# Gated attention and a ternary feed-forward on one Trainium2 core: a third pair of w1's row blocks rounded by GpSimd, and new orders for all queues

## What is computed

```python
# attention: x is (4, 512, 512), ctx is (4, 512, 128)
adj  = layernorm(x)
si   = ctx @ Wi ; sj = ctx @ Wj
xatt = 0.6 * sigmoid(si[:, :, None] + sj[:, None, :] + b) + 0.4 * adj
x    = x + tanh(g_xattn) * xatt
# feed-forward on quantized operands
def bitlinear(x, w):
    xn = x * rsqrt(mean(x * x) + 1e-6)
    s  = 127 / max(abs(xn)) ; xq = clip(round(xn * s), -128, 127) / s
    t  = 1 / mean(abs(w))   ; wq = clip(round(w * t), -1, 1) / t
    return xq @ wq.T
h = silu(bitlinear(layernorm(x), w1)) * bitlinear(layernorm(x), w2)
x = x + tanh(g_ffn) * bitlinear(h, w3)
```

## Time and profile before

| | |
|---|---|
| median of 3 runs | 155.48 us |
| profiled execution, its own time | 154.29 us |
| its span, first to last instruction | 152.5 us |
| PE busy | 137.5 us, 90% |
| DVE busy | 118.8 us, 78% |
| POOL busy | 107.6 us, 71% |
| ACT busy | 103.8 us, 68% |
| granted TensorE clock | 1.00 of full speed |
| moved by DMA | 27.94 MB, mean 183 GB/s |

### The profile page before, as it was taken

One profiled execution on the slowest core, in us unless ns is written; L12 is line 12 of the kernel. 1 busy time (PEld: TensorE's weight loads), 2 busy tenths in 40 slices (PEclk: granted clock), 3 DMA queues, 4 the chain that ended last, 5 costly groups with the idle time before them and its releaser, 6 DMA issues.

```text
span 152.5 us, 2380 instructions
## 1 busy us (share of the span) xinstructions
PE 137.5 (90%) x711; PEld 75.6 (50%) x711; DVE 118.8 (78%) x179; ACT 103.8 (68%) x172; POOL 107.6 (71%) x158
## 2 busy tenths in 40 slices
PE   1379568989999999799999999999999999999992
PEld 1279557955554444344444444445454454444461
DVE  0235998999999999979999999992779468908742
ACT  3148599999989778977597794283919719572250
POOL 3021297999898489894998969999742985699420
PEclk9999999999999999999999999999999999999999
DMA  4899999996129569980469519255802195819773
GB/s 122 229 409 406 410 407 426 404 384 217 34 71 142 129 149 237 204 158 21 78 130 232 94 37 141 63 152 149 198 2 89 43 185 111 232 69 227 184 217 138
DMA packets 46004, 27.94 MB, mean 183 GB/s; under 512 B 37543, under 2 KB 37928, under 8 KB 45992
## 3 DMA queue, kind: packets, MB, share of 16 engines
q1 hardware_dynamic: 45696, 27.79, 68.1%
q10 hardware_dynamic: 296, 0.01, 0.1%
HBM read 14.55 MB, written 4.20 MB: 123 GB/s over the span
## 4 chain that ended last, share of the span: by engine, by line
PE 72%; ACT 11%; DMA 6%; issue 5%; POOL 3%; ACTq 1%; SPq 1%; DVE 1%; DVEq 0%; POOLq 0%
PE ps L1404 42%; PE ps L1441 23%; ACT junk L720 3%; DMA th_ring<-in_L_xattn_b_dram 3%; DMA xqT<-xq 2%; POOL hq L587 2%; PE ps L1436 2%; ACT w2T L725 1%; PE ps L1310 1%; ACT w1T L730 1%; ACT th_ring L775 1%; ACT junk_x L792 1%; ACT raw_room L805 1%; PE ps L1317 1%; ACT hqT L736 1%
## 5 line engine op out<-in xcount | busy, mean ns | idle before, releaser
L1404 PE MATMUL ps<-w1T,xqT 128*128 128x512 f16 (+1 forms) x192 | 40.7, 361 | 0.9 <-DMA xqT<-xq 0.9
L1404 PE MATMUL ps<-w2T,xqT 128*128 128x512 f16 (+1 forms) x192 | 40.7, 362 | 0.0
L1125 DVE SCALAR_TENSOR_TENSOR raw<-ps,deq,raw_room 128x1408 f32<-128x1408 f32 x16 | 26.9, 1683 | 14.2 <-PE ps L1404 14.1
L1441 PE MATMUL ps<-w3T,hqT 128*128 128x512 f16 x165 | 37.2, 379 | 0.3 <-issue 0.3
L805 ACT ACTIVATE raw_room<-ps,deq 128x1408 f32<-128x1408 f32 x16 | 22.9, 1433 | 14.9 <-PE ps L1404 14.9
L1404 PEld LDWEIGHTS ps<-w1T,xqT 128*128 128x128 f16 x192 | 18.6, 98 | 20.9 <-issue 1.6
L1404 PEld LDWEIGHTS ps<-w2T,xqT 128*128 128x128 f16 x192 | 18.3, 98 | 20.1 <-DVE raw L1125 1.2
L1132 DVE TENSOR_REDUCE h_top<-raw 128x1 f32<-128x1409 f32 x16 | 25.7, 1607 | 0.1
L587 POOL TENSOR_SCALAR hq<-raw,h_scale 128x1408 f16<-128x1408 f32 x15 | 22.6, 1506 | 4.4 <-DVE h_scale L1135 4.4
L1441 PEld LDWEIGHTS ps<-w3T,hqT 128*128 128x128 f16 x165 | 16.1, 98 | 19.0 <-issue 0.7
L816 ACT ACTIVATE junk<-raw 128x1410 f16<-128x1410 f32 x16 | 21.8, 1368 | 0.0
(11 more groups left out here) (106 smaller groups left out, 180.2 us busy)
## 6 DMA issues: line engine op xcount, KB each, us to landing
c_all<-in_x_dram SPq DMA_DIRECT2D x16, 256.0 KB, 10.0
out_dram<-out_ring SPq DMA_DIRECT2D x15, 256.0 KB, 2.5
raw<-in_L_ffn_w_dram SPq DMA_DIRECT2D x4, 704.0 KB, 12.7
raw_room<-in_L_ffn_w_dram SPq DMA_DIRECT2D x3, 768.0 KB, 8.6
raw<-in_L_ffn_w_dram SPq DMA_DIRECT2D x3, 768.0 KB, 11.7
hq<-in_ctx_dram SPq DMA_DIRECT2D x2, 256.0 KB, 6.2
raw_room<-in_L_ffn_w_dram SPq DMA_DIRECT2D x1, 512.0 KB, 10.7
raw<-in_L_ffn_w_dram SPq DMA_DIRECT2D x1, 512.0 KB, 11.7
```

Of the source, the lines that this page charges most:

```text
L1125: v.scalar_tensor_tensor(out=hid[:, t % HS, 0:H], in0=ps_up[:, 0:H], scalar=deq[:, 1, t:t + 1], in1=gate[:, t % GATES, :], op0=ALU.mult, o ...
L1404: last = m.matmul(bank[:, lo:hi], xqT[:, i % XT, k, :], wT[w][:, k, lo:hi], start=(k == 0), stop=(k == KD - 1))
L1441: last = m.matmul(ps_y[t % 2], hqT[:, t % HT, k, :], w3T[:, :, k, :], start=(k == 0), stop=(k == KH - 1))
```

## The change

A third pair of row blocks, 5 and 6, joins the pairs that POOL rounds and PE turns as half floats. `RAW`, the number of blocks turned as 32-bit floats, goes from 7 to 5, the second clip of w1 shrinks from three blocks to one, and the room `w1q` grows by two blocks. PE's transposes for these blocks are eight of half floats in place of eight of 32-bit floats; ACT loses `evac_rows(5)`, DVE's `evac_rows(6)` becomes the eviction of a pair, and POOL gains one `conv_rows`. The order lists of all five queues are new.

```diff
-    ROWS = [(t, t + 1) for t in range(7)] + [(7, 9), (9, 11)]
-    RAW = 7
+    ROWS = [(t, t + 1) for t in range(5)] + [(5, 7), (7, 9), (9, 11)]
+    RAW = 5
     CLIPS = [(0, 4), (4, RAW)]
-    ROWS_ACT = [0, 4, 5]
-    ROWS_DVE = [1, 2, 3, 6, 7, 8]
+    ROWS_ACT = [0, 4]
+    ROWS_DVE = [1, 2, 3, 5, 6, 7]
...
@@ SP
             load_x(11)
+            turn_x(2)
             load_x(12)
-            turn_x(2)
-            turn_x(3)
...
@@ PE
-                            rows_left([6, 7, 8][c])
+                            rows_left([6, 7, 7][c])
...
+            up_product(1)
             sum_w(2, "x", 2)
-            up_product(1)
...
+            gate_product(7)
             last_product(0)
-            gate_product(7)
```

More of the change, by code:

```diff
@@ L620, in _ @@
             affine_x(2)
+            quant_x(1)
             affine_x(3)
-            quant_x(1)
+            dequant_up(0)
+            dequant_gate(0)
+            step_x(1)
             hidden_floors()
-            dequant_up(0)
-            step_x(1)
-            ctx_product(2)
             dequant_x(1)
             quant_x(2)
+            ctx_product(2)
             slopes_x(3)
@@ L631, in _ @@
             step_x(2)
+            quant_h(0)
+            dequant_x(2)
             conv_w(2, 0)
-            dequant_x(2)
+            quant_x(4)
             conv_w(2, 1)
-            quant_x(4)
-            conv_w(2, 2)
-            mean_x(0)
             quant_x(5)
             step_x(3)
+            conv_w(2, 2)
             dequant_x(3)
-            quant_h(0)
+            dequant_h(0)
+            quant_x(6)
+            mean_x(0)
+            conv_w(2, 3)
             quant_h(1)
-            quant_x(6)
-            conv_w(2, 3)
-            dequant_h(0)
             quant_x(7)
@@ L870, in _ @@
             evac_w(1, 4)
+            sum_w(2, 0)
+            evac_x(1)
+            silu(0)
             sum_w(2, 1)
-            silu(0)
-            evac_x(1)
+            sum_w(2, 2)
+            silu(1)
             square_x(2)
-            sum_w(2, 2)
             square_x(3)
-            score(5)
-            silu(1)
+            store_sj(2)
             score(6)
-            score(7)
             affine_x(4)
@@ L1215, in _ @@
             hidden(2)
-            sum_scores(2)
+            intercept(4)
+            weight_factor(2)
+            clip_w3(0)
+            max_h(1)
+            hidden(3)
             clip_w3(1)
             make_x(4)
-            hidden(3)
-            max_h(1)
+            clip_w3(2)
             max_x(4)
-            weight_factor(2)
             hidden(4)
-            clip_w3(2)
-            clip_w3(3)
-            max_h(2)
-            hidden(5)
             stats_x(5)
             stats_x(6)
+            clip_w3(3)
+            hidden(5)
+            max_h(2)
+            max_h(3)
+            max_h(4)
+            intercept(5)
+            sum_scores(3)
             hidden(6)
-            sum_scores(3)
-            intercept(5)
-            max_h(3)
+            intercept(6)
             make_x(5)
-            intercept(6)
             max_x(5)
-            max_h(4)
+            max_h(5)
             make_x(6)
-            max_h(5)
+            max_x(6)
+            stats_x(7)
             hidden(7)
-            stats_x(7)
-            max_x(6)
             stats_x(8)
-            hidden(8)
+            add_x(3)
             max_h(6)
             intercept(7)
+            hidden(8)
             affine_x(12)
+            affine_x(13)
+            max_h(7)
+            make_x(7)
             intercept(8)
-            affine_x(13)
+            max_x(7)
             hidden(9)
-            make_x(7)
-            add_x(3)
-            max_h(7)
-            max_x(7)
             max_h(8)
@@ L1463, in _ @@
             turn_w(1, 0)
-            turn_rows(8)
             turn_w(1, 1)
```

259 lines of the change are left out of this document (129 added, 130 removed).

## The result

The changed kernel takes 154.19 us, the median of four runs (153.70 to 154.37), against 155.49 for before (155.30 to 155.72) beside it: 0.991 of before, with an interval of 0.988 to 0.994. It is faster by 1.3 us, under 1%, where I forecast 156.2 and slower; the value lies just under the range. The profiled execution of the change took 154.11 us, with a span of 152.3.

A forecast was written before the change was run, and what follows sets the result against it. PE, busy nine tenths of the span, bounds the kernel by its product chain's start and pauses. Start 2.4 late less 1.64 won back is 0.8 slower: 156.2 from the median 155.48; own range 155.7 to 156.7, whole range 154.4 to 156.9.

The forecast's parts named there:

- the last one of the sum: Whole kernel: 155.1 against the profiled 154.29; that execution being 1.2 under the median, 156.2 from the median 155.48.
- The sum itself: Whole kernel: up_product(3) starts 2.4 late, 1.64 of PE's pauses is won back, so 0.8 slower.
- w1's and w2's scales: DVE's front end: w1's scale about 0.7 earlier, w2's no earlier, 26.9 against 26.73, with ACT running dry before evac_x(0).
- hidden(0): DVE, from w2's scale: 11.94 as before plus a hold of 0.3, so it starts at 39.15 against 38.67.
- The hold at `conv_w(1, 5)`: DVE, while POOL rounds w2: between nothing and 0.9 lost, taken as 0.3.
- hidden(1) and make_x(3): DVE: hidden(1) starts at 44.5; POOL rounds w3 from 46.75, 0.25 ahead of make_x(3), which loses 0.95.
- the pauses: PE, from up_product(3) to gate_product(7): eight products run without pause, winning back 1.64.
- up_product(3): PE: it starts at 52.35 against 49.93 before, 2.4 late.
- no hold at make_x(3): Rival, chance 0.26: DVE has its inputs before POOL rounds w3; up_product(3) is 1.45 late, time 155.3.
- the turns queue up: Rival, chance 0.09: SP's train of DMA turns lands w3's last row 1.5 later, up to 0.4 sticks out; 156.6.
- the front end comes early: Rival, chance 0.23: half_scores(1) early enough keeps ACT from running dry; w2's scale up to 0.9 earlier, time 154.4.

The follow-up runs named there:

- the lower group: The 23 of 75 runs of the unchanged kernel before, on three chips, that took under 154.6 us; their median is 153.41.
- the fourth profile of before: The kernel before, unchanged, profiled a fourth time; make_x(2) took 1.28 and the execution 154.06 us.
- before with DVE first: The kernel before plus one wait: ctx_product(2) on POOL waits until make_x(2) on DVE is done; median 153.45 us, before 155.10 on that chip.
- the fifth profile of the change: The changed kernel, unchanged, profiled again; one of six such further profiles, which took 153.13 to 154.06 us.
- the eight profiles: Eight profiled executions of the changed kernel, with no edit; the last six took 153.13 to 154.06 us, the first 154.11.
- the third of before: The kernel before, unchanged, profiled a third time; make_x(2) took 3.35 and the execution 158.0 us.
- before with POOL first: The kernel before plus one wait: make_x(2) on DVE waits until ctx_product(2) on POOL is done; median 157.49 us, before 155.10 on that chip.

## Why the prediction was wrong

**The step that failed** is the last one of the sum: "that execution was 1.2 under the median of the runs, so from the median, 155.48, I forecast 156.2". It treats the 1.2 as something that lies around any execution alike. It was a hold at `make_x(2)` that the profiled execution happened not to have, that by their times some two runs in three of before do have (52 of 75 lie above the lower group), and that the change makes impossible. Decided one way or the other by a wait, the meeting with all that follows from it is worth 4 us: 153.45 against 157.49. I had looked for meetings of POOL and DVE that the change adds, priced them from the earlier trace rows, and never asked which it takes away, although the move of `ctx_product(2)` stood in my own text. The trace that I had showed a sign: POOL's small instruction of 1.18 right ahead of it.

Without that step the sum still gives 155.1, 0.9 over the 154.19 measured. The profiled execution had no hold, but it was late: `spread_row` at 6.74 and w2's scale at 26.57, where six other executions with before's orders up to there have 4.92 to 5.66 and 24.64 to 25.41 (only the fourth profile of before is nearly as late, 6.56 and 26.39). Its 154.29 lies 0.9 above the median of the lower group, 153.41. So it was neither like the runs nor like their quick group. From 153.4 the sum of 0.8 would have given 154.2; that this meets the measured value so closely is luck, since 0.8 is itself some 0.3 too much.

**The sum itself** came out nearly right against its like, before without the hold: 154.05 against 153.45, on another chip, is 0.6 slower, where I summed 0.8; the quick runs on one chip, 153.87 (7 runs of the change) against 153.33 (the 10 of before's lower group), give 0.5. By its steps:

- *w1's and w2's scales*: w1's came earlier and w2's did not, as forecast. In the change w2's scale was at 25.49, with `spread_row` at 5.77; in before with DVE first at 25.41, with 5.57. ACT ran dry for 1.03 ahead of `evac_x(0)`, as forecast. That all this lay a microsecond ahead of my times goes with the first loads, which differ by the execution.
- *hidden(0)*: forecast 0.48 later. At a like start it was level, 37.84 in the fifth profile of the change (`spread_row` 5.50) and 37.85 in before with DVE first (5.57). There w2's scale was 0.19 earlier (25.22 against 25.41) and the way from it to `hidden(0)` 0.18 longer (12.62 against 12.44), where I had 0.17 later and 0.3 longer. The hold at `conv_w(1, 5)` is a matter of who is first: 0.4 to 0.7 in three of the eight profiles and none in five, so 0.3 is near their mean, 0.2, and right for no execution.
- *hidden(1) and make_x(3)*: from `hidden(0)` to `hidden(2)` 11.40, forecast 11.50, before 9.51. The hold was 0.95, as forecast. (My working has POOL ready for w3 at 46.5, and its terms add up to 46.4; nothing hangs on it, since POOL waited for w3's scale.)
- *the pauses*: the forecast of 1.64 won back holds but for 0.2. From `up_product(3)` to `gate_product(8)` PE took 31.13 (51.25 to 82.38), and 32.56 before (49.93 to 82.49): 1.43.
- *up_product(3)*: forecast 2.4 late; at a like start 1.9 (50.99 in the fifth profile of the change, 49.11 in before with DVE first). With 1.43 won back that leaves 0.5 slower, which is what the times show.
- *no hold at make_x(3)* and *the turns queue up* did not happen; *the front end comes early* gave a fitting time for a reason that was not there. For the turns I had set 3.6 us from issue to landing against a bandwidth; that time holds more than the transfer (in the change a plain 128 KB store took 1.9 by the same measure, a turned 128 KB 2.5), so those rows do not test it.

## What to carry to other kernels

When the profiled execution lies away from the median of its runs, find out what differs before adding the difference to a forecast; here a second and a third profile of the kernel before told more than the whole comparison. Where two engines can hold each other, list every pair that may meet, in the old order as well as in the new, and ask for each which comes first and by how much: a margin of 0.1 or 0.2 us went either way here, and a wait that makes the more critical engine first can be worth more than new orders.

## What the runs showed of the hardware

In the pairs that met here, one of VectorE and GpSimd stood still for nearly the whole of what was left of the other's instruction: `make_x(2)` of 1.27 took 3.22 and 3.35 behind a `ctx_product(2)` of 2.35, and GpSimd's small instruction of 0.19 took 1.18 behind `make_x(2)`. The Trainium skill says (Trainium Architecture — The Big Picture, What this means for kernel authors) that the port pair of the two is an exclusive lock and not a split of bandwidth; the trace agrees. An instruction with one input was held too: VectorE's `conv_w(1, 5)` of 0.48 took 0.91, 0.92 and 1.19 when GpSimd's rounding had begun first. What I had not expected is that such a pair can move a kernel's time by 2 us from one execution to the next.

A hold can be followed by a second loss: in two profiles (the third of before, and before with POOL first) the granted clock fell from 1.00 to 0.69 and 0.66 in 40 to 45 us, behind a wait of PE of 1.83, and `up_product(1)` took 4.24 and 4.08 in place of 2.55. In another execution the same wait was followed by the full clock.
